# Routing a mixture of experts tile by tile, with places that need no totals

## The chip, the cores and the metric

The kernel runs on one core of a Trainium2 chip. The metric is the device time of one execution in microseconds. Before the change it is 1632.67 us, the median of three runs (1632.34 to 1632.82). The engines are named as in the profile: PE is TensorE, DVE is VectorE, ACT is ScalarE, POOL is GpSimd, SP is SyncE, which here only issues DMAs.

## What is computed

The input is 4096 tokens of 128 numbers (4 sequences of 1024), all in float32. Four parts follow one another:

```python
a = L0_attn(x)                    # linear attention, LayerNorm, gated FFN of width 341, LayerNorm
m = a + sum_e down_e(silu(a @ Wg_e) * (a @ Wu_e))   # 8 experts, all of them for each token, width 512
z = layernorm(m)                  # "n3": input of the second half
z4 = four layers(z)               # each: LayerNorm, quaternion products, filter, projection, LayerNorm, MLP of width 512
bid = sigmoid(z @ conf_w.T + conf_b) * wealth       # router: 8 numbers a token
top 2 of bid, weights softmax(bid[top 2])
y = sum over the 2 chosen e of weight * down_e(silu(z @ gate_e.T) * (z @ up_e.T))
out = m + z4 + y
```

The last part, the routed experts, needs only z and the router's numbers and not the result of the four layers, so the two can run side by side. With two experts a token there are 8192 rows to be computed, sorted by expert.

## The kernel before, in words

The tokens lie transposed in SBUF (feature on the partition, token along the row), in 8 tiles of 512 (`TILES`); a tile is 4 groups of 128 tokens (`GROUPS`). A planner written in the file decides the order of the work: `schedule` declares every step with the engines that it uses, a length in us, an urgency and the steps that it must follow (`step(...)`), some with resources that one step takes and another gives back (banks 6 and 7, the buffers YF and XS, the ACT table). `Plan.run` lays out the steps and gives each engine a fixed order. At run time each engine goes through its own order and waits on semaphores; nothing is reordered. The constants in capitals (NORM3, START, LATE, PACE) set urgencies, in units of one expert step.

*First stage, 256 expert steps.* For each tile, 32 steps (8 experts of 4 chunks): gate and up products of one chunk (L1231 to L1233, three passes each), silu on ACT (L780), product on DVE (L1110), down product into bank 4 (L1243). Between them lies the attention of the first half and, from the first finished tile on, the four layers of each tile: the products on DVE are `ham` (L1003 is the first of 13, L1009 to L1020 the others), the last addition of a layer is L1206.

*Normalisation.* `scaling` is used for every LayerNorm: PE centres four groups (L1321), ACT squares them (L789), POOL takes the power -0.5 (L953, step `power`), ACT copies the four groups scaled into rows of tokens (L802, step `scale`), PE turns them back (L1327, step `turn`). For the kind `n3` the rows are written to ROWS3, which is the buffer YF; SP stores them into the DRAM tensor xrows (step `rows`, L676), and only then is YF free for `ffn2_add` of the next tile. PE forms the router's logits from z (L1374), ACT copies them into LG (L865), 32 columns a tile.

*Routing, once for all tokens.* After tile 7, `route` runs for all 4096 tokens on DVE with 256 columns an operation (L1041 to L1062: bias, sigmoid by a Tanh on ACT, best and second best of 8). Each DVE operation is tied to the one before by `link` (a semaphore). PE counts how often each expert is chosen and ranks each token within its expert (L1415 to L1426). DVE turns the totals into the end of each expert's share, in blocks of 256 rows (`BLOCK`), and from end and rank into PLACE, the row of each token and choice (L1065 to L1079), then into OWNER, the expert of each of the 39 blocks (L1081 to L1084), then the weights. SP loads the rows of all tokens back from xrows into TOKROWS, and `columns` adds to each row its destination and its weight. POOL scatters them (step `scatter`, L959): 64 indirect DMAs of 128 rows of 520 bytes into the DRAM tensor xg, whose 9984 rows SP has filled with empty rows beforehand in three transfers (step `fill`, L671).

*Last stage, 39 blocks.* SP loads a block's weights by the expert in OWNER (`load_w`, behind the semaphore `placed`) and its 256 rows (`load_x`, behind all 64 scatters). PE transposes the rows (`turn_in`, L1436), ACT copies them, PE forms gate and up (L1447), ACT silu, DVE product, PE down (L1458), ACT scales by the weight, POOL scatters the results to ytok by the destination in the row (L970). After the last block, `load_y`, `back` (L1468), `merge` (L1222) and `out` bring them into the output, tile by tile.

## Time and profile before

| | us |
|---|---|
| median of 3 runs | 1632.67 |
| lowest, highest | 1632.34, 1632.82 |
| profiled execution, its time | 1633.69 |
| profiled execution, its span | 1631.9 |
| PE busy | 1478.9 (91% of the span) |
| DVE busy | 1144.5 (70%) |
| ACT busy | 1021.3 (63%) |
| POOL busy | 339.9 (21%) |
| DMA | 208.74 MB, 128 GB/s on average |

The span is the time between the first and the last instruction that the profiler saw; the profiled execution's own time is 1.8 us longer. Busy shares are averages over stages: which engine sets the time must be read stage by stage, from the slices and windows. The slices cut the span into 40 pieces of 40.8 us. The granted clock is what the chip allowed PE in that stretch; 1.00 is its upper level, 2.4 GHz, and values in between are a mix with the lower one, 1.2 GHz.

### The profile page before, as it was taken

To read this page: it belongs to the slowest core of one execution; us is meant where nothing else is said; L and a number is where in the kernel's file an instruction comes from. 1 tells how busy PE (TensorE), PEld (TensorE's weight loads), DVE (VectorE), ACT (ScalarE), POOL (GpSimd) and SP (SyncE) were. 2 spreads that over 40 slices of the span, in tenths; PEclk is the share of its full clock that TensorE was granted. 3 is DMA by queue.
4 is the path that set the end of the run, shared out by engine and by line. 5 is a ranking of instruction groups with operands and counts; after the bars stand their busy time and mean duration, and the time that the engine had idled before them with its cause. 6 is when DMAs were issued, how large, how long until landed. Compare 5 with 4: busy or idle time off the path is not lost.

```text
span 1631.9 us, 20218 instructions
## 1 busy us (share of the span) xinstructions
PE 1478.9 (91%) x6166; PEld 975.7 (60%) x6166; DVE 1144.5 (70%) x1222; ACT 1021.3 (63%) x2447; POOL 339.9 (21%) x253
## 2 busy tenths in 40 slices
PE   6999999998999999999999999996656999999996
PEld 4766566565555655555565566553323667677885
DVE  3433745948999359947993899799888798857221
ACT  6455657568666684677667667566636876655430
POOL 0001001101101111100011011013887233344231
PEclk9999999999999999999999999998769999999998
DMA  5733343334344244243432434325423354445455
GB/s 204 268 123 118 118 159 105 115 112 159 107 126 131 87 115 131 84 122 100 126 100 89 137 103 121 108 68 173 112 73 90 115 149 146 144 129 177 145 162 164
DMA packets 114853, 208.74 MB, mean 128 GB/s; under 512 B 13815, under 2 KB 61772, under 8 KB 113452
## 3 DMA queue, kind: packets, MB, share of 16 engines
q1 hardware_dynamic: 110204, 198.09, 39.7%
q0 software_dynamic: 4544, 9.38, 1.7%
q8 instruction: 51, 0.84, 0.2%
q14 instruction: 54, 0.44, 0.1%
HBM read 158.20 MB, written 29.24 MB: 115 GB/s over the span
## 4 chain that ended last, share of the span: by engine, by line
PE 34%; issue 28%; DVE 14%; ACT 12%; POOL 11%; DMA 1%; POOLq 0%; SPq 0%; ACTq 0%; DVEq 0%
PE bank L1243 6%; PE bank L1231 4%; PE bank L1233 4%; PE bank L1232 4%; POOL xg L959 4%; POOL ytok L970 4%; POOL RSTD L953 3%; PE bank L1409 3%; ACT ROWS L789 3%; PE bank L1321 3%; DVE TA L1009 2%; PE bank L1403 2%; DVE SH L1110 2%; DVE AM L1013 2%; DVE AM L1017 2%
## 5 line engine op out<-in xcount | busy, mean ns | idle before, releaser
L953 POOL TENSOR_TENSOR RSTD<-SS,power_half 128x4 f32<-128x4 f32 x96 | 139.4, 1452 | 952.4 <-ACT ROWS L789 952.1
L1110 DVE TENSOR_TENSOR SH<-SH,bank 128x512 f32<-128x512 f32 x256 | 172.8, 682 | 154.7 <-ACT SH L780 109.3
L1231 PE MATMUL bank<-NH,GU 128*128 128x512 f32 x512 | 266.9, 521 | 5.1 <-DVE SH L1110 2.9
L1243 PE MATMUL bank<-SH,WD 128*128 128x512 f32 x512 | 261.5, 593 | 0.1
L1009 DVE TENSOR_TENSOR TA<-QK 128x2048 f32<-128x2048 f32 x96 | 219.6, 2287 | 1.3
L780 ACT ACTIVATE SH<-bank 128x512 f32<-128x512 f32 x256 | 151.4, 601 | 110.0 <-PE bank L1233 106.7
L789 ACT ACTIVATE ROWS<-bank,root_eps 128x128 f32<-128x128 f32 x384 | 135.8, 367 | 123.4 <-PE bank L1321 123.1
L1233 PE MATMUL bank<-NL,GU 128*128 128x512 f32 x512 | 204.1, 399 | 0.0
L1232 PE MATMUL bank<-NH,GU 128*128 128x512 f32 x512 | 203.2, 397 | 0.0
L802 ACT ACTIVATE ROWS<-bank,RSTD 128x128 f32<-128x128 f32 x384 | 109.8, 372 | 78.1 <-POOL RSTD L953 72.0
L1013 DVE TENSOR_TENSOR AM<-AM,TA 128x1024 f32<-128x1024 f32 x128 | 152.9, 1217 | 0.6
L1447 PE MATMUL bank<-XT,GU 128*128 128x256 f32 x624 | 146.7, 381 | 3.3 <-ACT XT L929 3.3
L970 POOL DMA_INDIRECT ytok<-YS,XR x78 | 97.9, 1255 | 212.4 <-ACT YS L941 199.8
L1403 PE MATMUL bank<-XS,FC 128*128 128x512 f32 x256 | 126.5, 617 | 11.2 <-ACT GE L916 8.2
L1231 PEld LDWEIGHTS bank<-NH,GU 128*128 128x128 f32 x512 | 97.2, 190 | 54.6 <-issue 34.7
L1447 PEld LDWEIGHTS bank<-XT,GU 128*128 128x128 f32 x624 | 113.7, 190 | 20.8 <-ACT XT L929 5.0
L1232 PEld LDWEIGHTS bank<-NH,GU 128*128 128x128 f32 x512 | 98.0, 191 | 45.6 <-issue 33.2
L1215 DVE TENSOR_TENSOR SH<-SH,bank 128x512 f32<-128x512 f32 x78 | 52.9, 683 | 101.3 <-PE bank L1447 54.3
L1409 PE MATMUL bank<-GE,MP 128*128 128x512 f32 x256 | 119.2, 610 | 2.4 <-ACT GE L916 2.0
L1383 PE MATMUL bank<-XS,WQ 128*128 128x512 f32 x192 | 99.2, 626 | 14.7 <-ACT QK L877 11.7
L1243 PEld LDWEIGHTS bank<-SH,WD 128*128 128x128 f32 x512 | 96.6, 189 | 24.9 <-DVE SH L1110 0.9
L1233 PEld LDWEIGHTS bank<-NL,GU 128*128 128x128 f32 x512 | 96.6, 189 | 22.6
(197 smaller groups left out, 2492.7 us busy)
## 6 DMA issues: line engine op xcount, KB each, us to landing
GU<-halves SPq DMA_DIRECT2D x112, 512.0 KB, 3.9
GU<-in_w_gu SPq DMA_DIRECT2D x39, 512.0 KB, 3.7
WD<-in_w_d SPq DMA_DIRECT2D x128, 128.0 KB, 2.2
QK<-QK SPq DMA_DIRECT2D x32, 480.0 KB
WD<-in_w_d SPq DMA_DIRECT2D x39, 256.0 KB, 3.9
halves<-GU SPq DMA_DIRECT2D x8, 1024.0 KB, 6.3
FC<-ready_w SPq DMA_DIRECT2D x32, 256.0 KB, 3.9
MP<-in_w_mproj SPq DMA_DIRECT2D x32, 256.0 KB, 4.0
```

What stands on the lines that cost most here:

```text
L789: ins = act.activation(ROWS[:, i, :], LNB[:, i * P:(i + 1) * P], ACT.Square, bias=root_eps[:], scale=P ** -0.5, accum_out=SS[:, i:i + 1])
L953: pool.tensor_tensor(RSTD[:], SS[:], (power_one if k[0] == "at" else power_half)[:], ALU.pow).then_inc(power_done, 1)
L970: pool.indirect_dma_start(ytok, bass.IndirectOffsetOnAxis(ap=to, axis=0), YS[:, g % 2, j, :], None).then_inc(y_stored[i], 16)
L1009: ins = dve.tensor_tensor(TA[:], q, k_(1 + i // 3), ALU.mult)
L1013: ins = dve.tensor_tensor(pair(AM, *d), pair(AM, *d), pair(TA, *s), op)
L1110: dve.tensor_tensor(SH[:, g % 4, :], SH[:, g % 4, :], banks[2 + g % 2][:], ALU.mult).then_inc(h_ready, 1)
L1231: pe.matmul(out, w_hi, x_hi, start=True, stop=False)
L1232: pe.matmul(out, w_lo, x_hi, start=False, stop=False)
L1233: return pe.matmul(out, w_hi, x_lo, start=False, stop=True)
L1243: pe.matmul(banks[4][:], WD1[:, slot, :], SH[:, g % 4, :], start=first, stop=last).then_inc(down_done, 1)
L1409: mm = pe.matmul(banks[7][:], MP[:, c, :], GE[:, c, :], start=(c == 0), stop=(c == 3))
L1447: mm = pe.matmul(banks[bank][:, c * BLOCK:(c + 1) * BLOCK], GU[:, g % DEEP, a:a + P], XT[:, i, :], start=True, stop=True)
```

## The change

Each tile is routed as soon as its logits are there (step `route` with the tile in its key, four stages), and its 8 indirect DMAs go out at once. To need no totals, each expert gets 4096 rows of its own in xg (`c_base`, loaded into OFF, is expert number times 4096). BASE, the next free row of each expert, starts there and grows by the tile's counts; a token's place is BASE plus its rank in the tile. The ranks are 4 accumulating matmuls of 32 columns (one with the triangle `tri`, three with ones for the groups before), and 4 of 8 columns give the tile's totals. The Exp of the weights stays on ACT, once a tile. ACT writes the n3 rows twice, into SEND0 (in YF) and into SEND, one copy for each choice, each with room for its destination and weight; xrows, TOKROWS, `columns`, `load_rows` and the tables btri and of_expert are gone. xg has 34560 rows and not 9984; SP fills it in 8 transfers of 4096 rows, each before its tile's scatters, and a last one of 1792 rows. YF is free for the next tile's `ffn2_add` when the tile's 8 scatters have landed. After tile 7, `block_table` computes on DVE from the totals which expert each block has (OWNER) and at which row of xg it begins (ROW0), behind a small load of block numbers that SP issues after the last routing; `load_x` reads the start from there into a register. The last stage waits for these and for all scatters. The planner gets the new steps and lengths and other values for some of its constants; `prep` (the layers' weights) is put at other places.

The core of the diff:

```diff
+            step("power", k, urgency, [(POOL, 1.4)], [("centre", k, ACT_)])
+            step("scale", k, urgency, [(ACT_, 2.0 if kind == "n3" else 1.0, ("YF",) if kind == "n3" else ())], [("power", k, POOL)])
...
-    for i in range(-(-BLOCKS * BLOCK // TOK)):
-        step("fill", i, SPAN * (i + 2), [(SP, 0.1)], [("expert", (i + 2, 0), PE)])
+    for t in range(TILES):
+        step("fill", t, SPAN * t - 18, [(SP, 0.1)], [("expert", (t - 1, 4), PE) if t else ("raw", EXPERTS - 1, SP)])
...
-    ATTN = (-7.31, 18.93)
-    NORM1 = (2.85, 60.26)
-    FFN2 = (67.27, -54.82)
-    NORM2 = (29.18, 38.61)
-    NORM3 = (-31.42, 13.09)
+    ATTN = (-7.21, 18.93)
+    NORM1 = (4.12, 60.26)
+    FFN2 = (67.27, -48.32)
+    NORM2 = (9.93, 112.4)
+    ROUTE = (4.0, 3.97)
+    NORM3 = (-32.06, -2.73)
...
-             [("ffn2", (t, c), DVE) for c in range(3)] + last("ffn2_down", PE) + ([("rows", t - 1, SP, 3.0)] if t else []))
+             [("ffn2", (t, c), DVE) for c in range(3)] + last("ffn2_down", PE) + ([("scatter", (t - 1, 7), POOL, 3.0)] if t else []))
...
-        step("rows", t, a + NORM3[h], [(SP, 0.1, (), ("YF",))], [("turn", ("n3", t), PE)])
...
+        step("logits", t, a + NORM3[h] + 4.0, [(PE, 0.9, ("6",)), (ACT_, 0.1, (), ("6",))],
+             [("normed", ("n3", t), ACT_)] + ([("route", (t - 1, 3), DVE)] if t else []))
+        r = a + NORM3[h] + ROUTE[h]
+        step("route", (t, 0), r, [(DVE, 0.15), (ACT_, 1.4, ("table",), ("table",))], [("logits", t, ACT_)])
+        step("route", (t, 1), r, [(DVE, 3.3)], [("route", (t, 0), ACT_)])
+        step("route", (t, 2), r, [(PE, 1.4, ("6",)), (ACT_, 1.4, ("table",), ("table",), (), -1.4)], [("route", (t, 1), DVE)])
+        step("route", (t, 3), r, [(DVE, 2.5, (), ("6",))], [("route", (t, 2), ACT_), ("route", (t, 2), PE)])
+        for i in range(2 * GROUPS):
+            step("scatter", (t, i), r + 0.01 * i, [(POOL, 1.45, (), ("YF",) if i == 7 else ())],
+                 [("route", (t, 3), DVE), ("fill", t, SP, 14.0)])
...
-    LATE, PACE = 236.33, 2.81
-    ROUTE = -500.0
-    step("load_rows", 0, ROUTE, [(SP, 0.3)], [("rows", TILES - 1, SP, 3.0), ("logits", TILES - 1, ACT_)])
...
-    step("route", 3, ROUTE, [(PE, 0.9)], [("route", 2, ACT_, -2.4)])
-    step("route", 4, ROUTE, [(DVE, 6.0)], [("route", 3, PE), ("route", 2, ACT_)])
-    step("route", 5, ROUTE, [(POOL, 0.3)], [("scatter", NG - 1, POOL, 2.5)])
-    for j in range(2 * NG):
-        step("scatter", j, ROUTE + 0.01 * j, [(POOL, 1.6)], [("load_rows", 0, SP, 12.0), ("route", 5, POOL) if j >= NG else ("route", 4, DVE)])
+    LATE, PACE = 236.33, 0.74
+    step("load_numbers", 0, -500, [(SP, 0.1)], [("route", (TILES - 1, 3), DVE)])
+    step("table", 0, -500, [(DVE, 4.9)], [("load_numbers", 0, SP, 2.5)])
...
+        step("load_w", g, u - 9, [(SP, 0.8)], [("table", 0, DVE)] + ([("down", g - DEEP, PE)] if g >= DEEP else []))
+        step("load_x", g, u - 3, [(SP, 0.4)], [("table", 0, DVE), ("scatter", (TILES - 1, 7), POOL, 3.0)] + ([("y_store", (g - DEEP, 1), POOL, 2.0)] if g >= DEEP else []))
...
+    xg = nc.dram_tensor("xg", (SENT, P + 2), F32, kind="Internal").ap()
...
-                at = slice(k * TOK, min((k + 1) * TOK, BLOCKS * BLOCK))
-                sp.dma_start(xg[at, :], A["c_fill"][at, :]).then_inc(filled, 16)
+                if k >= 2:
+                    sp.wait_ge(filled[k % 2], 16 * (k // 2))
+                some = [x[0:EXPERTS * TOK, :].rearrange("(e r) n -> e r n", e=EXPERTS)[:, k * TILE:(k + 1) * TILE, :]
+                        for x in (xg, A["c_fill"])]
+                sp.dma_start(*some).then_inc(filled[k % 2], 16)
+                if k == TILES - 1:
+                    sp.dma_start(xg[EXPERTS * TOK:, :], A["c_fill"][EXPERTS * TOK:, :]).then_inc(rest_filled, 16)
...
-            elif name == "rows":
-                sp.wait_ge(rows_scaled, upto("scale", ("n3", k)))
-                sp.dma_start(xrows[k * TILE:(k + 1) * TILE, :].rearrange("(g p) n -> p g n", p=P), ROWS3[:]
-                             ).then_inc(rows_stored, 16)
...
-                sp.wait_ge(rows_stored, 16 * TILES)
-                sp.dma_start(TOKROWS[:, :, 0:P], xrows.rearrange("(j p) n -> p j n", p=P)).then_inc(tokrows_loaded, 16)
+            elif name == "load_numbers":
+                sp.wait_ge(routed, TILES)
+                sp.dma_start(block_no[:], A["c_block_no"][:, 0:BLOCKS]).then_inc(numbers_loaded, 16)
...
                 sp.wait_ge(scattered, 16 * 2 * NG)
+                sp.wait_ge(rest_filled, 16)
+                sp.wait_ge(table_set, 1)
                 if k >= DEEP:
                     sp.wait_ge(x_turned, k - DEEP + 1)
                     sp.wait_ge(y_stored[i], 16 * 2 * (k // DEEP))
-                sp.dma_start(XR[:, i, :, :], xg[k * BLOCK:(k + 1) * BLOCK, :].rearrange("(i p) n -> p i n", p=P)
+                r = sp.value_load(ROW0[0:1, k:k + 1], min_val=0, max_val=SENT - BLOCK)
+                sp.dma_start(XR[:, i, :, :], xg[bass.ds(r, BLOCK), :].rearrange("(i p) n -> p i n", p=P)
                              ).then_inc(xr_loaded[i], 16)
...
-                    dst = ROWS3
-                    act.wait_ge(rows_stored, 16 * k[1])
+                    dst = SEND0
+                    act.wait_ge(scattered, 16 * 2 * GROUPS * k[1])
                     act.wait_ge(centred, upto("centre", ("n2", k[1])))
                 act.wait_ge(turned_back, n)
                 for i in range(GROUPS):
-                    ins = act.activation(dst[:, i, :], LNB[:, i * P:(i + 1) * P], ACT.Copy, scale=RSTD[:, i:i + 1])
+                    ins = act.activation(dst[:, i, 0:P], LNB[:, i * P:(i + 1) * P], ACT.Copy, scale=RSTD[:, i:i + 1])
+                    if k[0] == "n3":
+                        ins = act.activation(SEND[:, i, 0:P], LNB[:, i * P:(i + 1) * P], ACT.Copy, scale=RSTD[:, i:i + 1])
                 ins.then_inc(rows_scaled, 1)
...
-                pool.wait_ge(filled, 16 * -(-BLOCKS * BLOCK // TOK))
-                pool.wait_ge(tokrows_loaded, 16)
-                i, j = k // NG, k % NG
-                pool.wait_ge(columns_set, i + 1)
-                pool.indirect_dma_start(xg, bass.IndirectOffsetOnAxis(ap=PLACE[:, i, j:j + 1], axis=0),
-                                        TOKROWS[:, j, :], None).then_inc(scattered, 16)
-            elif name == "route" and k == 5:
-                pool.wait_ge(scattered, 16 * NG)
-                columns(pool, 1)
+                t, i = k
+                c, g = i // GROUPS, i % GROUPS
+                pool.wait_ge(filled[t % 2], 16 * (t // 2 + 1))
+                pool.wait_ge(routed, t + 1)
+                rows = SEND0 if c == 0 else SEND
+                pool.indirect_dma_start(xg, bass.IndirectOffsetOnAxis(ap=PLACE[:, c, g:g + 1], axis=0),
+                                        rows[:, g, :], None).then_inc(scattered, 16)
...
+            elif stage == 3:
+                dve.wait_ge(ranked, t + 1)
+                rank = banks[6][:, 0:GROUPS * EXPERTS].rearrange("p (g e) -> p g e", e=EXPERTS)
+                link(dve.tensor_tensor(SLOT[:], rank, wide(BASE[:]), ALU.add))
+                total = banks[6][:, GROUPS * EXPERTS:(GROUPS + 1) * EXPERTS]
+                dve.tensor_tensor(BASE[:], total, BASE[:], ALU.add).then_inc(rank_read, 1)
+                link(dve.tensor_tensor(PICKED[:], ONE[:], SLOT[:].unsqueeze(1).broadcast_to([P, 2, GROUPS, EXPERTS]), ALU.mult))
                 link(dve.tensor_reduce(PLACEF[:], PICKED[:], AX.X, ALU.add))
+                dve.wait_ge(scattered, 16 * 2 * GROUPS * t)
+                dve.wait_ge(rows_scaled, upto("scale", ("n3", t)))
                 dve.tensor_copy(PLACE[:], PLACEF[:])
-                shape = [1, BLOCKS + 1, EXPERTS]
-                link(dve.tensor_tensor(PAST[:], block_no[:].unsqueeze(2).broadcast_to(shape),
-                                       end[0:1, EXPERTS:].unsqueeze(1).broadcast_to(shape), ALU.is_ge))
-                link(dve.tensor_reduce(OWNERF[:], PAST[:], AX.X, ALU.add))
-                dve.tensor_scalar(OWNER[:], OWNERF[:], EXPERTS - 1.0, None, ALU.min).then_inc(placed, 1)
-                dve.wait_ge(exp_done, 1)
+                for c, rows in ((0, SEND0), (1, SEND[:])):
+                    dve.tensor_copy(rows[:, :, P].bitcast(mybir.dt.uint32), dest[:, c, t * GROUPS:(t + 1) * GROUPS])
+                dve.wait_ge(exp_done, t + 1)
                 link(dve.tensor_scalar(SUM[:], EX[:], 1.0, None, ALU.add))
-                link(dve.reciprocal(WEIGHT[:, 0, :], SUM[:]))
-                link(dve.tensor_tensor(WEIGHT[:, 1, :], EX[:], WEIGHT[:, 0, :], ALU.mult))
-                columns(dve, 0)
+                link(dve.reciprocal(SEND0[:, :, P + 1], SUM[:]))
+                dve.tensor_tensor(SEND[:, :, P + 1], EX[:], SEND0[:, :, P + 1], ALU.mult).then_inc(routed, 1)
...
+        def block_table():
+            dve.wait_ge(numbers_loaded, 16)
+            dve.wait_ge(rank_read, TILES)
+            for e in END:
+                dve.memset(e[:], 0.0)
+            link(dve.tensor_tensor(FILL[:], BASE[:], OFF[:], ALU.subtract))
+            link(dve.tensor_scalar(FILL[:], FILL[:], 1.0 / BLOCK, (BLOCK - 1.0) / BLOCK - 0.5 + 0.5 / BLOCK, ALU.mult, ALU.add))
+            link(dve.tensor_scalar(FILL[:], FILL[:], ROUND, None, ALU.add))
+            link(dve.tensor_scalar(FULL[:], FILL[:], ROUND, None, ALU.subtract))
+            link(dve.tensor_copy(END[0][:, EXPERTS:], FULL[:]))
+            for i, d in enumerate((1, 2, 4)):
+                a, b = END[i % 2], END[(i + 1) % 2]
+                link(dve.tensor_tensor(b[:, EXPERTS:], a[:, EXPERTS:], a[:, EXPERTS - d:2 * EXPERTS - d], ALU.add))
+            link(dve.tensor_scalar(FILL[:], FULL[:], -float(BLOCK), float(TOK), ALU.mult, ALU.add))
+            shape = [1, BLOCKS, EXPERTS]
+            link(dve.tensor_tensor(PAST[:], block_no[:].unsqueeze(2).broadcast_to(shape),
+                                   END[1][0:1, EXPERTS:].unsqueeze(1).broadcast_to(shape), ALU.is_ge))
+            link(dve.tensor_tensor(SKIP[:], PAST[:], FILL[0:1, :].unsqueeze(1).broadcast_to(shape), ALU.mult))
+            link(dve.tensor_reduce(OWNERF[:], PAST[:], AX.X, ALU.add))
+            link(dve.tensor_reduce(ROW0F[:], SKIP[:], AX.X, ALU.add))
+            link(dve.scalar_tensor_tensor(ROW0F[:], block_no[:], float(BLOCK), ROW0F[:], ALU.mult, ALU.add))
+            dve.tensor_copy(ROW0[:], ROW0F[:])
+            dve.tensor_scalar(OWNER[:], OWNERF[:], EXPERTS - 1.0, None, ALU.min).then_inc(table_set, 1)
...
-                dve.wait_ge(rows_stored, 16 * k)
+                dve.wait_ge(scattered, 16 * 2 * GROUPS * k)
...
+            elif name == "route":
+                pe.wait_ge(chosen, k[0] + 1)
+                bank_free(pe, 6, name, k)
+                out = banks[6][:, 0:GROUPS * EXPERTS]
+                every = ones[:, 0:1].broadcast_to([P, P])
+                pe.matmul(out, tri[:], CHOSEN[:, GROUPS - 1:, :].rearrange("p g e -> p (g e)"), start=True, stop=False)
+                for d in range(1, GROUPS):
+                    at = slice(GROUPS - 1 - d, 2 * GROUPS - 1 - d)
+                    pe.matmul(out, every, CHOSEN[:, at, :].rearrange("p g e -> p (g e)"), start=False, stop=(d == GROUPS - 1))
+                for g in range(GROUPS):
+                    mm = pe.matmul(banks[6][:, GROUPS * EXPERTS:(GROUPS + 1) * EXPERTS], every, CHOSEN[:, GROUPS - 1 + g, :],
+                                   start=(g == 0), stop=(g == GROUPS - 1))
                 mm.then_inc(ranked, 1)
...
-                pe.wait_ge(placed, 1)
+                pe.wait_ge(o_added, TILES)
```

## Rows read from the trace of the kernel before

**Rows 1.** The page, busy tenths and granted clock in 40 slices of the span.

```profile
PE   6999999998999999999999999996656999999996
...
PEclk9999999999999999999999999998769999999998
```

**Rows 2.** Windows: length, then busy us and instructions of each engine, clock, DMA share, GB/s.

```profile
0.00:1100.00 1100.00, 1034.52 (x4078) 661.36 (x4078) 777.11 (x841) 723.96 (x1731) 111.53 (x85) 1.00 0.40 124
...
900.00:1100.00 200.00, 190.90 (x696) 116.85 (x696) 177.54 (x178) 131.93 (x321) 20.51 (x14) 0.99 0.37 110
...
1140.00:1270.00 130.00, 83.64 (x218) 38.13 (x217) 114.67 (x98) 73.14 (x183) 101.42 (x71) 0.80 0.35 98
1270.00:1600.00 330.00, 314.73 (x1633) 241.89 (x1632) 211.20 (x220) 197.35 (x459) 114.34 (x88) 1.00 0.47 143
```

**Rows 3.** Lines L959 (scatters) and L1436 (transposes of blocks): min/median/max ns, first and last start.

```profile
L959 POOL DMA_INDIRECT xg<-TOKROWS,PLACE x64: 955/1055/2971, 1132.0 to 1260.3; - x64
...
  issue: 17.1, 59
...
DMA to landing us min/median/max: 2.3/3.2/7.3
...
L1436 PE MATMUL bank<-ident,XR x78: 272/273/327, 1269.0 to 1592.4; 128*128 128x128 f32 x78
```

**Rows 4.** Timeline of the last tile's scaling, logits and routing: start us, us, engine, line.

```profile
1104.38 1.14 ACT L802 ACTIVATE attn_raw<-bank,RSTD 128x128 f32<-128x128 f32 x4 [0.16 <-POOL RSTD L953]
...
1107.92 0.96 PE L1374 MATMUL bank<-conf,Z 128*128 128x8 f32 x8
...
1109.80 0.21 ACT L865 ACTIVATE LG<-bank 128x32 f32<-128x32 f32 x1
...
1116.33 0.19 DVE L1057 TENSOR_TENSOR DIF<-M 128x32 f32<-128x32 f32 x1
...
1125.96 0.57 DVE L1071 TENSOR_TENSOR END<-END 128x8 f32<-128x8 f32 x3
```

**Rows 5.** Block loads, last block matmuls, layer products (L1003) and a layer's last addition (L1206).

```profile
XR<-xg SPq DMA_DIRECT2D x39, 130.0 KB, 2.3
...
L1458 PE MATMUL bank<-WD,SH x624: 272/275/377, 1287.9 to 1601.2; 128*128 128x128 f32 x156
...
1131.02 2.29 DVE L1003 TENSOR_TENSOR AM<-QK 128x2048 f32<-128x2048 f32 x1
...
1419.47 2.29 DVE L1003 TENSOR_TENSOR AM<-QK 128x2048 f32<-128x2048 f32 x1 [0.34 <-ACT V L907]
...
1483.18 2.29 DVE L1003 TENSOR_TENSOR AM<-QK 128x2048 f32<-128x2048 f32 x1 [0.94 <-ACT V L907]
...
L1206 DVE SCALAR_TENSOR_TENSOR Z<-bank,LC,Z x32: 737/746/753, 235.9 to 1534.4; 128x512 f32<-128x512 f32 x32
```

**Rows 6.** ACT's table loads, and what PE waited for (whole span, to 1100, 1130 to 1270).

```profile
101.64 1.28 ACT L780 ACT_TABLE_LOAD   x1
102.94 1.09 ACT L780 ACTIVATE SH<-bank 128x512 f32<-128x512 f32 x2
...
L780 ACT ACT_TABLE_LOAD x36 | 46.2, 1283 | 0.6
...
L925 ACT ACT_TABLE_LOAD x1 | 1.3, 1283 | 0.0
...
L1231 PE MATMUL bank<-NH,GU 128*128 128x512 f32 x512 | 266.9, 521 | 5.1 <-DVE SH L1110 2.9 <-ACT SH L780 2.2
...
PE bank L1327 <- ACT ROWS L802: 20.3, 21, 6.5
...
PE bank L1327 <- ACT ROWS L802: 21.8, 8, 6.5
```

**Rows 7.** The fills: their size and landing time, and the window behind the first one.

```profile
xg<-in_c_fill SPq DMA_DIRECT2D x2, 2080.0 KB, 10.4
...
225.00:235.00 10.00, 10.00 (x33) 5.62 (x32) 2.54 (x4) 8.27 (x17) 1.01 (x1) 1.00 0.91 319
```

195 lines of the change are left out of this document (70 added, 125 removed).

## The prediction

> **What bounds the kernel now.** The slices come first [rows 1]: TensorE (PE) reads 9 almost everywhere, except in the first slice, in slices 28 to 31 (about 1101 to 1264 us), where it reads 6, 6, 5, 6 and the granted clock falls to 7 and 6, and in the last. TensorE is the bound; there is one hole. The windows give it numbers [rows 2]: from 0 to 1100 us PE is busy 1034.5 of 1100 us (94.0%), from 1270 to 1600 us 314.7 of 330 (95.4%), but from 1140 to 1270 us only 83.6 of 130, at a mean granted clock of 0.80. Next, the one line that runs in the hole and nowhere else [rows 3]: 64 scatters on POOL, the first at 1132.0 us, the last at 1260.3, and the first transpose of a block of the last stage at 1269.0. No block of that stage may start before all 64 have landed, and they cannot start before all eight tiles are routed. In the meantime PE has only the attention layers, a chain that VectorE (DVE) carries: it is busy 114.7 of the 130 us. So the hole is not spare time of a slow engine. It is matmul work of 39 blocks, locked behind POOL's scatters, while PE idles. What ends last there is the scatter chain.
>
> **What the change does to the hole.** Of 64 scatters, 56 move to where their tiles are finished, before 1100 us; 8 are left behind the last tile. I build the new start of the last stage from the old times of the last tile. Its logits reach SBUF at 1109.8+0.2 us [rows 4]. The scaling in front of them issues eight copies where it issued four; four take 1.14 us [rows 4], so +1.1. Routing is then 16 DVE operations up to CHOSEN; one of 32 columns took 0.19 us, and three small linked ones 0.57 [rows 4]; at 0.20 us that is 3.2. The ranks are 8 matmuls, each two instructions in the trace; the logits' matmuls, as narrow, took 0.96 us for 8 instructions [rows 4], so 1.9 for 16. Ten DVE operations follow, 2.0. Eight scatters at 0.96 us and 0.30 of issue [rows 3] take 10.1; landing is 3.2 [rows 3], the load of a block 2.3 [rows 5]. With 1 us for handovers that is 1134.8. DVE is in order and its layer operations of 2.29 us stand between the routing steps [rows 5]: two of them, 4.6. First block at about **1140 us instead of 1269**. The block table (about 20 DVE operations, some 5 us) and the first weights behind it lie beside the scatters. If that cover is gone, they cost those 5 us once.
>
> From there the remaining PE work is the same. Full-clock work is busy time times granted clock: 83.6 x 0.80 = 66.9 us in the rest of the hole, and 314.7 up to 1600 us, together 381.6 [rows 2]. At the 95.4% of the late stage this takes 400.1 us, so the last block's last matmul, at 1601.5 us now [rows 5], comes at 1140 + 400.1 + 1.5 = 1541.6. The tail behind it (last stores, load back, transposes, output) does not change. **Term A: -60 us.** Does DVE allow it? It has 114.7 + 211.2 = 326 us to do in 401 us, 81%. From 900 to 1100 us it ran at 89% with PE at 95% [rows 2], so yes. The layers' last addition is at 1534.4 us now [rows 5], and need not come sooner. Ten of the eleven layers left start their products from 1131.0 to 1419.5 us [rows 5], on average 32 us apart: 29 in the hole (four steps up to 1247.4), 34.4 beside blocks. The last starts 64 us later and ends 51 after that. At 34.4 throughout it ends at 1131 + 9 x 34.4 + 64 + 51 = 1555.6. Behind the layers come some 15 us of output, behind the blocks 30 (1601.5 to 1631.9), so the two ends are even. The bounds of A are -65 (PE at 97%) and -45 (layers late by 15 us).
>
> **What the change adds before 1100 us.** PE: the ranks, 16 instructions and 1.92 us for each of 7 tiles, 13.4 us on the engine that is the bound. They are no filler for idle time, since that time is waits at handovers of an ordered queue. **Term B: +13.4 us** (bounds 0, all in gaps, and 14).
>
> ScalarE: four more copies a tile (1.1 us), one Tanh, one Exp. The Tanh of now has no table load in the trace; the Exp has one [rows 6]. So I count two loads a tile (Exp, and silu again), 14 in all. A load lasts 1.283 us, and the copy after it starts 0.02 us behind its end [rows 6]. PE waited 2.9 + 2.2 us in all for the silu and its product, with 36 returns to silu [rows 6], 0.14 us each: 14 x 0.14 = 2.0. The Trainium skill ("ScalarE: Activation LUTs", section "What ACT_TABLE_LOAD costs") says that a switch costs the 1.283 us and a drain of 1.38 us besides. By it the 14 switches would hold ScalarE 37 us and not 18; the trace has the load as stated and no gap behind it, so the sum goes without the drain.
>
> POOL: 56 scatters of 1.26 us. POOL is busy 111.5 of 1100 us [rows 2], so there is room, but its other work is the power step in the middle of every normalisation, and PE's transpose waits behind that: 20.3 us in 21 waits up to 1100 us [rows 6]. A power caught behind one scatter is late by 1.26 us at most; I take one or two a tile, half of it passed on: 7 x 0.6 = 4. The doubled copies lengthen one of the tile's normalisations by 1.1 us; about every third of them makes PE wait (21 waits, some 80 normalisations), so 7 x 1.1 x 0.3 = 2. **Term C: +8 us** (2 + 4 + 2). Its lower bound is 0. Its upper bound is the hole: there PE waited 21.8 us for ROWS beside 64 scatters [rows 6], so 19 for 56; with all the added copies (8) and 2 for tables, 29.
>
> DVE: 26 operations a tile at 0.2 us, 5.2 us, 37 us in seven tiles; it is busy 777 of 1100 us, 71%, and becomes 74%. Nothing, while it stays under the 89% that it has from 900 to 1100 us [rows 2]. Against that the 12 us of routing 4096 tokens at once near 1110 to 1131 us shrink to 5.
>
> DMA: the empty rows written beforehand grow from 5.2 to 18 MB, in eight fills of 2.1 MB, where there were two [rows 7] and a short one. I cost them at nothing: in the window right behind the first fill the DMA share was 0.91 and PE was busy 10.00 of 10 us [rows 7], as weights are loaded several steps ahead. A fill takes 10.4 us to land [rows 7]; if that cover is gone (the first one falls into the start-up), 5 to 10 us once. The 8 row stores, the reload of 2 MB and the five tables behind it go away; the first block's load waits no more for them. On SyncE each block gets one register load more, 39 in all, hidden behind a block's matmuls (some 6 us).
>
> **Sum.** -60 + 13.4 + 8 = -38.6 on the profiled execution (1633.69 us, its span 1631.9). The median of the runs shown is 1632.67, a microsecond lower; from it, **1594 us**.
>
> **Rivals.**
>
> *Costs hidden.* B and C fall into the 65 us of PE's idle time before 1100 us, and A reaches -63: 1632.7 - 63 = 1570. For it: the planner orders the steps and can put ranks where PE waits. Against: PE has waits of 1 to 2 us there, each already in a dependency. Chance 0.14.
>
> *The hole closes only in part.* The layers become the bound after 1140 us: two chains of four layers each, DVE at 81%, and their short matmuls now queue on PE among those of the blocks. If they come every 37 us, the last addition is at 1131 + 9 x 37 + 64 + 51 = 1579, the end some 15 us later, 1594; B and C, which shift all of it, make 1615. For it: 34.4 us apart beside blocks, and 64 for the last. Against: there they had room to wait, since the blocks set the end. Chance 0.15.
>
> *Slower, by buffer YF.* The rows of a tile now lie in YF until its eight scatters have landed; before, a single store of them freed it. The next tile's ffn2_add on DVE waits for them, and behind it in DVE's queue stand the experts' products, hence PE. The planner knows of this, with 1.45 us a scatter; in the hole the longest took 2.97 [rows 3]. Where scatters run 1.5 us long, a tile's eight are 12 us late. From 5.5 us of stall a tile on (38.6 / 7) the gain is gone; at 10 us, 1594 + 70 = 1664. For it: POOL's work did stretch in the hole. Against: a tile lasts 137 us, in which 10 to 25 us of scatters find room, and POOL idled there 90%. Chance 0.05.
>
> *The last stage does not start early.* A wait keeps it (the last fill, the rows' order), or the order written by the planner puts layer steps first, and only B and C (+21.4) are left against what a POOL free of scatters can return of PE's waits for ROWS in the hole (-21.8, [rows 6]): 1632, within 0.2%. Chance 0.04; 0.62 stays for the forecast.
>
> **How the numbers follow.** The forecast's own range is 1577 to 1610 (A and C within two thirds of their bounds). The whole range of 8 in 10 reaches down to the first rival and into the second: 1567 to 1620. A difference of 0.2%, 3.3 us, is about what a measurement of this kernel can tell from no change. Faster by more: 0.62 + 0.14 + 0.15, and a bit of the last, 0.92; the same 0.02; slower 0.06.
>
> **What would show it.** Right: 56 scatters spread over 130 to 1090 us and 8 near 1120 to 1132; first block transpose at about 1160 (B and C shift it by some 20 us); granted clock 9 in every slice but the last; last block matmul near 1560; ranks at 1.9 us a tile. Wrong in A: layers' last addition behind the last block, PE idle beside it. Wrong in C: in the waits, PE for ROWS well above 25 us before 1100, or DVE waiting for the scatters. Wrong in DMA: PE waiting for weights.

## The result, and the profile after

Four runs of the changed kernel gave a median of 1597.62 us (1592.25 to 1601.19), four of the kernel before beside them 1632.74 us: a ratio of 0.977, with a 95% interval of 0.974 to 0.979 (the quotient of the two medians, 0.9785, lies inside it). The forecast of 1594 us is 4 us off. Its parts are not as good as their sum. The profiled execution of after took 1592.25 us (span 1590.4), 5 us under its median; the runs of this kernel spread more than those of before (9 us against 4), so the windows below explain a difference of 41.5 us between two spans, and the medians one of 35. Times in this document are medians of executions at the usual granted clock (a mean of 0.96 to 0.99 over the span), and two slower ones, of scat2 (2172 us at 0.65) and of the kernel before beside it (1692 us at 0.88), are left out.

The page of the changed kernel, its busy time and the slices that answer to [rows 1]:

```profile
span 1590.4 us, 20945 instructions
...
PE 1480.2 (93%) x6278; PEld 988.1 (62%) x6278; DVE 1167.9 (73%) x1414; ACT 1039.9 (65%) x2503; POOL 341.8 (21%) x251
...
PE   6999999999999999999999999999779999999978
...
PEclk9999999999999999999999999999889999999989
```

The hole of four slices has become one of two, 7 and 7. A dip in the granted clock is left there (8 and 8), and there is a new soft spot at the very end, 7 and 8 with a clock of 8 and 9.

The windows of after, cut at its last experts' addition (1111.4 us; the addition that ends the first stage's expert work for tile 7), its first block transpose (1179.8) and its last block matmul (1535.3); the columns are those of [rows 2]:

```profile
0.00:1111.40 1111.40, 1050.94 (x4192) 678.70 (x4192) 800.00 (x1020) 743.64 (x1782) 186.39 (x141) 0.99 0.42 136
1111.40:1179.80 68.40, 47.91 (x151) 24.84 (x152) 58.08 (x90) 44.85 (x122) 19.10 (x14) 0.80 0.36 107
1179.80:1535.30 355.50, 340.79 (x1745) 258.01 (x1744) 276.17 (x274) 236.04 (x562) 131.24 (x92) 1.00 0.48 146
1535.30:1590.40 55.10, 40.53 (x195) 26.59 (x193) 33.64 (x35) 15.35 (x39) 5.03 (x4) 0.90 0.43 133
```

And the kernel before, cut at the same event of its own, its last experts' addition at 1099.3 us, and at its first block transpose:

```profile
0.00:1099.30 1099.30, 1034.15 (x4077) 661.23 (x4078) 776.41 (x840) 723.67 (x1730) 111.53 (x85) 1.00 0.40 124
1099.30:1269.00 169.70, 110.23 (x317) 54.19 (x316) 150.38 (x155) 98.64 (x254) 112.04 (x78) 0.81 0.39 111
```

These windows divide the difference in two. By the last experts' addition both kernels have done nearly the same layer work (the last additions of 19 layers lie before it in both), and after is 12.1 us late. From there to the end of the span before needs 532.6 us (1631.9 - 1099.3) and after 479.0: 53.6 us less. 12.1 - 53.6 = -41.5, the difference of the spans. The prediction had +21.4 and -60.

Four lines of after, with the first and last start of each: the additions of the experts, the blocks' transposes, the blocks' last matmuls (down product), and the layers' last additions.

```profile
L1119 DVE SCALAR_TENSOR_TENSOR X<-bank,cols,X x8: 742/746/751, 126.6 to 1111.4; 128x512 f32<-128x512 f32 x8
...
L1440 PE MATMUL bank<-ident,XR x78: 272/273/330, 1179.8 to 1515.3; 128*128 128x128 f32 x78
...
L1462 PE MATMUL bank<-WD,SH x624: 272/275/423, 1193.5 to 1535.3; 128*128 128x128 f32 x156
...
L1211 DVE SCALAR_TENSOR_TENSOR Z<-bank,LC,Z x32: 739/744/752, 239.9 to 1585.7; 128x512 f32<-128x512 f32 x32
```

In before the blocks ended 66.8 us behind the layers [rows 5]. Now the layers end 50.4 us behind the blocks, and the span ends 4.7 us after their last addition.

### The profile page after: what moved, and what is told of

It is laid out like the page before. It is cut to its first block, busy times and chain, and to the rows that moved or that the text cites. A ratio compares the mean times of both kernels' runs of the same rounds, so it can differ in the third digit from the quotient of the medians.

```text
span 1590.4 us, 20945 instructions
## 1 busy us (share of the span) xinstructions
PE 1480.2 (93%) x6278; PEld 988.1 (62%) x6278; DVE 1167.9 (73%) x1414; ACT 1039.9 (65%) x2503; POOL 341.8 (21%) x251
## 3 DMA queue, kind: packets, MB, share of 16 engines
q1 hardware_dynamic: 105020, 206.60, 41.5%
## 4 chain that ended last, share of the span: by engine, by line
PE 43%; issue 19%; DVE 15%; ACT 15%; POOL 4%; DMA 3%; SPq 1%; POOLq 0%; ACTq 0%; DVEq 0%
PE bank L1250 6%; PE bank L1416 4%; PE bank L1238 4%; PE bank L1240 4%; PE bank L1239 4%; PE bank L1410 4%; PE bank L1328 3%; ACT ROWS L781 3%; POOL RSTD L945 2%; PE bank L1451 2%; ACT ROWS L794 2%; DVE AM L1003 2%; PE bank L1390 2%; DVE SH L1115 2%; DVE TA L999 2%
## 5 line engine op out<-in xcount | busy, mean ns | idle before, releaser
L1115 DVE TENSOR_TENSOR SH<-SH,bank 128x512 f32<-128x512 f32 x256 | 171.8, 682 | 129.0 <-ACT SH L772 89.2
L772 ACT ACTIVATE SH<-bank 128x512 f32<-128x512 f32 x256 | 151.4, 602 | 98.6 <-PE bank L1240 95.9
L1003 DVE TENSOR_TENSOR AM<-AM,TA 128x1024 f32<-128x1024 f32 x128 | 153.0, 1218 | 0.8
L960 POOL DMA_INDIRECT ytok<-YS,XR x78 | 108.5, 1390 | 162.2 <-ACT YS L933 149.2
L1334 PEld LDWEIGHTS bank<-ident,ROWS 128*128 128x128 f32 x384 | 45.3, 144 | 88.0 <-ACT ROWS L794 71.1
```

The costliest lines, as they stand in the source:

```text
L1003: ins = dve.tensor_tensor(pair(AM, *d), pair(AM, *d), pair(TA, *s), op)
L1115: dve.tensor_tensor(SH[:, g % 4, :], SH[:, g % 4, :], banks[2 + g % 2][:], ALU.mult).then_inc(h_ready, 1)
```

## Where the last tile's time goes

The forecast put the first block 41 us behind the last experts' addition; it came 68.4 us behind. The timeline of after in that stretch (start, duration, engine, line):

```profile
1111.36 0.74 DVE L1119 SCALAR_TENSOR_TENSOR X<-bank,cols,X 128x512 f32<-128x512 f32 x1
...
1119.15 2.08 PE L1328 MATMUL bank<-centre,X 128*128 128x128 f32 x8 [1.02 <-ACT XS L827]
...
1128.62 0.68 ACT L819 ACTIVATE Z<-bank 128x512 f32<-128x512 f32 x1
1128.96 3.67 PE L1416 MATMUL bank<-GE,MP 128*128 128x512 f32 x8 [0.59 <-ACT GE L910]
...
1136.33 0.20 ACT L860 ACTIVATE LG<-bank 128x32 f32<-128x32 f32 x1 [0.41 <-PE bank L1381]
...
1144.57 0.19 DVE L1052 TENSOR_TENSOR CHOSEN<-ONE 128x32 f32<-128x32 f32 x1
...
1149.96 0.38 PE L1424 MATMUL bank<-CHOSEN,tri 128*128 128x32 f32 x2
...
1153.36 0.17 DVE L1070 TENSOR_TENSOR SEND<-EX,attn_raw 128x4 f32<-128x4 f32 x1
...
1155.78 1.06 POOL L952 DMA_INDIRECT xg<-attn_raw,PLACE  x1 [0.18 <-issue]
...
1166.98 0.96 POOL L952 DMA_INDIRECT xg<-SEND,PLACE  x1 [0.30 <-issue]
...
1174.25 4.43 SPq L724 DMA_DIRECT2D XR<-xg  x4
...
1179.78 0.38 PE L1440 MATMUL bank<-ident,XR 128*128 128x128 f32 x2
```

The durations of most single operations are as forecast: 0.16 to 0.22 us on DVE, 1.9 us for the ranks. A scatter took 0.96 to 1.95 us where 0.96 was counted; in [rows 3] that is the shortest, the median is 1.055. Step by step:

| stretch | measured, us | counted, us |
|---|---|---|
| addition to logits in SBUF (1136.5) | 25.2 | 11.8 |
| to CHOSEN (1144.8) | 8.2 | 3.2 |
| to the first rank matmul (1149.96) | 5.2 | 0 |
| to the first scatter (1155.78) | 5.8 | 3.9 |
| to the end of the eighth scatter (1167.94) | 12.2 | 10.1 |
| to the load of the blocks' rows (1174.25) | 6.3 | 3.2 |
| to the first transpose (1179.78) | 5.5 | 2.3 |
| handovers, and DVE's layer work between the steps | in the rows above | 5.6 |
| sum | 68.4 | 40.1 (40.7 with 1139.4 rounded to 1140) |

What the sum lacked is mainly time in queues. After's written order puts a layer's centring, projections and transposes ahead of the tile's own centring (1119.15), and more of a layer's products ahead of the logits. DVE does layer operations between the routing steps, for which the 5.6 us were meant. From CHOSEN to the ranks PE does projections of a layer and waits for its ROWS. The first scatter stands behind a power operation of a layer on POOL. The last transposes ahead of the first block wait 2.3 us for a layer's ROWS, while the block's rows had landed 2.2 us after their issue. Such queues make 28.7 us more in five of the rows (13.4 + 5.0 + 5.2 + 1.9 + 3.2), against the 5.6 that were allowed: 23.1 of the 27.7 us missed. The rest is the scatters' length (2.1) and the landing of the last one (3.1, less 0.6 of rounding). SP stood 3.5 us waiting for that landing:

```profile
SPq L723 <- DMA xg<-SEND,PLACE: 3.5, 1, 3.5
```

The forecast counted 3.2 us for it, and it took about 6. Just before it SP had issued the weights of the first four blocks (3.1 MB, 1164.23 to 1169.44 us), and from 1168 to 1174 us the DMA engines were busy all the time, at 357 GB/s. No run moved these loads, so that they delayed the landing is likely and not shown.

## Experiments

All ratios are to the kernel before on the same chip, with 95% intervals. A kernel that was to price the doubled copies of the n3 rows (copy2, four more ACT copies a tile) needs more SBUF than there is and has no time, so their cost by itself is not measured.

**late100: does the gain come from the early start?** The schedule is told that the numbers for the block table arrive 100 us later. It writes its orders by that, and nothing else changes.

```diff
...
-    step("table", 0, -500, [(DVE, 4.9)], [("load_numbers", 0, SP, 2.5)])
+    step("table", 0, -500, [(DVE, 4.9)], [("load_numbers", 0, SP, 102.5)])
```

> The kernel after, where the planner is told that the block table is ready 100 us later, so that the order of each engine has layer steps first and the blocks start about as late as before the change; all instructions and waits are the same. If the early start of the blocks is the gain (term A, 60 us) and the early routing costs the 12 us by which the last experts' addition came later (1111 against 1099), this gives back the gain and keeps the cost: 1635-1655. Rival 'POOL free of scatters speeds the layers up in the hole' : the layers run faster without scatters, and it stays at 1600-1625.

Measured: 1657.18 us, ratio 1.012 [1.009, 1.015]. The experts' last addition was at 1110.3 us, as in after; the blocks' lines:

```profile
L1440 PE MATMUL bank<-ident,XR x78: 272/273/473, 1286.2 to 1617.8; 128*128 128x128 f32 x78
...
L1462 PE MATMUL bank<-WD,SH x624: 272/275/377, 1311.1 to 1626.7; 128*128 128x128 f32 x156
```

The first block starts 106.4 us later than in after and the last matmul ends 91.4 us later. So with a late start the gain is gone; it is the start of the blocks, as term A said. That POOL without scatters might speed the layers up in the hole is refuted: the hole is there again (PE busy 116.0 of the 175.9 us between the experts' last addition and the first block), with POOL busy for only 32.1 us of it. The loss of some 20 us is more than the 12 us of the change's early cost, and 2 us above the expected range: the first block came 17.2 us later than in before (1286.2 against 1269.0).

**pace281 and pace16: which end sets the time?** The change also set PACE, the distance at which blocks are due in the schedule, from 2.81 to 0.74 us.

```diff
-    LATE, PACE = 236.33, 0.74
+    LATE, PACE = 236.33, 2.81
```

That is pace281, which takes the value of before; pace16 has 1.6 there and pace18 (below) 1.8.

> The kernel after, with the planner's PACE back at 2.81 (0.74 after the change); it gives the blocks less urgency against the layer steps, and touches nothing else. In the profile of after the blocks end at 1535 us and the layers' last addition only at 1586, so I now hold that the layers set the end. Theory 'layers bound the end': the last addition moves forward to about 1530-1545, the blocks' last matmul back to about 1555-1565, the whole gains 5 to 15 us on after (about 1583-1592). Rival 'PE's work bounds the end': the two ends swap places and the time stays within 3 us of after, 1598. Rival 'planner constants carry the gain': it loses, 1605 or more.

> The kernel after with PACE 1.6, between the two. Theory 'layers bound the end': both ends come within 20 us of each other, and the time is the lowest of the three, 1580-1588. Rival 'PE's work bounds the end': within 3 us of after.

pace281: 1612.27 us, 0.986 [0.984, 0.987]; pace16: **1587.58 us, 0.971 [0.969, 0.972]**, below the changed kernel's 0.977 [0.974, 0.979]. The expectation for pace281 failed: the ends moved as its first theory said (layers' end earlier, blocks' end later) but the blocks' end overshot, to 1577.2 and not 1565, and the time rose by 15 us where it was to fall by 5 to 15. It lies in the range of the third theory, that the new planner constants carry part of the gain; see oldplan. Their ends, blocks' last matmul and layers' last addition:

```profile
L1462 PE MATMUL bank<-WD,SH x624: 272/275/421, 1190.5 to 1577.2; 128*128 128x128 f32 x156
...
L1211 DVE SCALAR_TENSOR_TENSOR Z<-bank,LC,Z x32: 739/744/753, 240.6 to 1547.0; 128x512 f32<-128x512 f32 x32
```

```profile
L1462 PE MATMUL bank<-WD,SH x624: 272/275/377, 1191.6 to 1553.3; 128*128 128x128 f32 x156
...
L1211 DVE SCALAR_TENSOR_TENSOR Z<-bank,LC,Z x32: 739/744/751, 239.3 to 1563.2; 128x512 f32<-128x512 f32 x32
```

The first fence is pace281, the second pace16; in both the blocks set the end, in pace16 by 15 us, in after the layers do. Each span is the later of two ends, by a rule read off these traces: the blocks' last matmul plus 30 us, or the layers' last addition plus 5 us. pace281 gives 1577.2 + 30 = 1607 (span 1607.6), pace16 1553.3 + 30 = 1583 (1582.6), after 1585.7 + 5 = 1591 (1590.4). The rule fits within 2 us in every trace of this document.

> The changed kernel with PACE 1.8 instead of 0.74, that is blocks due 1.8 us apart. If the end is set by the later of the blocks' last matmul plus 30 us and the layers' last addition plus 5 us, the trace of PACE 1.6 (blocks 1553.3 us, layers 1563.2 us) has the blocks' end as the later one already, and more pace moves the blocks later still: 1588 to 1600 us. If the balance still leans to the layers there, 1580 to 1586 us.

pace18 gave 1590.54 us, 0.974 [0.971, 0.977]. Its blocks ended earlier than with 1.6, at 1546.1, and its layers later, at 1584.1 (+ 5 = 1589, span 1588.8). The rule held; the expectation that a larger PACE moves the blocks later was wrong: the time is in its range, but the other end makes it. The planner lays out many steps one after another, and a small change of one constant moved the ends either way.

**rank2: what do the rank matmuls cost?** They are issued twice.

```diff
+                for twice in range(2):
-                pe.matmul(out, tri[:], CHOSEN[:, GROUPS - 1:, :].rearrange("p g e -> p (g e)"), start=True, stop=False)
+                    pe.matmul(out, tri[:], CHOSEN[:, GROUPS - 1:, :].rearrange("p g e -> p (g e)"), start=True, stop=False)
...
```

> The kernel after with each tile's 8 rank matmuls issued twice (16 instructions and 1.9 us more a tile, same result). If term B is a full cost on the bound engine, the last experts' addition comes 7 x 1.9 = 13 us later (1124) and the whole 13-15 us later (1611-1613). If PE's idle time before 1100 us takes them in, the addition moves by under 5 us and so does the whole.

1617.19 us, 0.988 [0.986, 0.991], 4 us above the expected range. The window up to its last addition:

```profile
0.00:1131.40 1131.40, 1072.09 (x4304) 698.10 (x4304) 800.17 (x1019) 743.27 (x1782) 182.55 (x141) 0.98 0.42 133
```

Against the window of after the addition is 20.0 us later and PE 21.15 us busier, for 112 more instructions (16 in each of seven tiles) that cost 13.4 us at full clock. Idle time absorbed next to nothing of it (59.3 us idle, 60.5 in after). The other 7.7 us, which the expectation lacked, go with a lower granted clock (mean 0.98 against 0.99). Cut the first 1100 us into windows of 10 us, and for each multiply its 10 us by what its granted clock lacks to 1.00: the sum, time lost by the clock, is 3.5 us in before, 8.5 in after and 17.1 in rank2. A cluster of ranks often stands behind a pause of PE; the section on the hardware shows one.

**only8: what does the hole cost by itself?** The kernel before, with 8 of its 64 scatters (56 are left out, so most rows of the blocks are empty ones; the blocks compute as long as ever) and a write of 4 MB to the outputs' buffer ahead of time.

```diff
...
-    for j in range(2 * NG):
+    for j in range(8):
...
```

> The kernel before, with 8 of the 64 scatters (the other 56 left out, so most tokens get no routed experts; the places they would have been read from are filled beforehand, 4 MB more); the blocks all run, on mostly empty rows, and the planner knows of the 8. Nothing is added before 1100 us. Theory 'the 56 scatters behind tile 7 are what holds the blocks': the first block comes at about 1160 and not 1269, and the time is 1565-1580, the gain of term A alone. Rival 'something else holds the blocks' (the reload of all rows, the weights, the order): under 20 us of gain, 1613 or more.

1589.77 us, 0.974 [0.971, 0.978]. First block at 1168.8 us instead of 1269.0, blocks' end at 1556.3 instead of 1601.5, the layers' last addition at 1543.0. The first block is 100 us earlier and the blocks' end 45: term A measured without the rest of the change. (The last addition is at 1106.2 us, 6.9 later than in before: PE has one wait of 7.7 us more, up to 394.5 us. The profile names no releaser for it; the added write went out at 366.0.) Behind that addition the kernel needs 480.2 us (1586.4 - 1106.2) instead of 532.6: the early start by itself is worth 52.4 us, nearly the 53.6 of the change. Its expectation, 1565 to 1580 us, was too low, by about as much as the first block was later than the 1160 us expected; 6.9 us of that are the addition's delay.

**scat2, scat15, scat2plan: do the scatters hold up the normalisations?** Every scatter is sent a second time, to a spare buffer; in scat15 only those of the first choice (c == 0); in scat2plan all, and the schedule is told, which is the second hunk.

```diff
+                pool.indirect_dma_start(xg2, bass.IndirectOffsetOnAxis(ap=PLACE[:, c, g:g + 1], axis=0),
+                                        rows[:, g, :], None).then_inc(spare, 16)
...
-            step("scatter", (t, i), r + 0.01 * i, [(POOL, 1.45, (), ("YF",) if i == 7 else ())],
+            step("scatter", (t, i), r + 0.01 * i, [(POOL, 2.9, (), ("YF",) if i == 7 else ())],
```

> The kernel after with each of the 64 scatters issued twice, the second time into another DRAM tensor (10 us more of POOL a tile; the planner does not know). Theory 'early scatters hide in POOL's idle time': the last experts' addition stays within 3 us of 1111, and only the last tile's 8 scatters show, 10 us: 1603-1610. Rival 'scatters hold up the normalisations' (the cost put at 4 us in term C, or the YF rival): the addition moves by 10 us or more, and the whole to 1615 or more.

> The changed kernel with the scatters of the first choice alone sent twice, the second time to a spare buffer: 12 scatters a tile instead of 8 (16 a tile moved the last experts' addition from 1111.4 us to 1170.5 us). If each scatter in front of a power operation costs the layer normalisations the same amount, the addition moves by half of that, to about 1141 us, and the time by about 30 us, to 1627 us; and then the 8 scatters that the change itself makes would have cost about 59 us, which its trace does not have. If POOL has room for the scatters up to some number and only more than that holds TensorE up, the cost is bent: under 12 us, an addition before 1124 us and a time of 1600 to 1612 us.

> The changed kernel with each scatter sent twice, as in scat2, and the schedule's scatter step told to last 2.9 us instead of 1.45, so that the written orders of POOL and TensorE are made for the doubled scatters. scat2 without this had its last experts' addition at 1170.5 us, 59 us behind the changed kernel, and TensorE waited 61.6 us for the scaled rows before 1100 us. If what the doubled scatters cost is POOL's time itself, the addition stays behind 1155 us and the waits for the scaled rows above 45 us. If it is that the order of the other engines was made for scatters of half the length, the addition comes back to 1110 to 1125 us, the waits to under 30 us, and the scatters of the change, which its schedule knows, cost next to nothing before the last addition. The time would then be 1600 to 1625 us (16 scatters of tile 7 lie ahead of the first block, and the ends of blocks and layers shift with the order).

scat2: 1656.91 us (three executions), 1.016 [1.012, 1.020], last addition at 1170.5. scat15: 1631.39 us, 0.997 [0.995, 0.999], addition at 1143.8. scat2plan: 1635.45 us, 1.000 [0.998, 1.002], addition at 1126.1. What PE waited for, up to 1100 us in after and scat2 and up to 1110 in scat2plan (us in total, times, longest):

```profile
PE bank L1334 <- ACT ROWS L794: 17.9, 21, 6.7
```

```profile
PE bank L1342 <- ACT ROWS L798: 61.6, 22, 10.0
```

```profile
PE bank L1342 <- ACT ROWS L798: 23.5, 15, 6.0
```

The line is PE's transpose waiting for rows that ACT scaled by POOL's power. scat2 refutes that early scatters always hide in POOL's idle time: sent without the schedule's knowledge they hold the normalisations up. Such scatters cost in proportion: 4 more a tile moved the addition by 32 us, 8 more by 59. So the bent cost that scat15 was to show isn't there, and the consequence that the change's own 8 scatters cost 59 us too isn't in the trace either. scat2plan tells why. With the same doubled scatters in a schedule that knows them, the waits fall from 61.6 to 23.5 us and the addition comes back by 44 of 59 us (1 us short of the expected range). It is the fixed order of the engines, made for shorter scatters, that costs most, not POOL's time. The whole kernel comes back by less, 21 of the 59 us between scat2 and the changed kernel, and missed its expected 1600 to 1625 us. Before the last stage PE stood 18.15 us in front of the first block, whose rows now lie behind 16 scatters of the last tile, and the layers' last addition came at 1627.6.

```profile
1197.46 0.69 PE L1448 MATMUL bank<-ident,XR 128*128 128x128 f32 x2 [18.15 <-DMA XR<-xg]
```

**oldplan: where is the cost that was forecast?** The changed kernel with the due times of before for the steps that both have: NORM2 as shown, and NORM0, KEYS, KV_SUM, ATTN, NORM1, FFN2, NORM3 and START likewise.

```diff
...
-    NORM2 = (9.93, 112.4)
+    NORM2 = (29.18, 38.61)
...
```

> The changed kernel with the due times of the kernel before for the steps that both have (NORM0, KEYS, KV_SUM, ATTN, NORM1, FFN2, NORM2, NORM3, START). If the 4.7 us of idle TensorE time that the change had less before the last experts' addition came from its new due times, that idle time is back and more: the addition at 1120 to 1132 us, TensorE idle for 70 us or more before it (60.5 us in the changed kernel), and a time of 1603 to 1615 us. If it came from the structure (no reload of the rows, no split of the chain), the addition stays at 1111 us within 3 us and the time within 5 us of 1595 us.

1614.5 us, 0.986 [0.982, 0.991]: a ratio 0.010 above the changed kernel's, 16 us. The last addition came at 1140.0 us, later than either theory had it, with PE idle for 67.9 us before it (1140.0 - 1072.13):

```profile
0.00:1140.00 1140.00, 1072.13 (x4253) 691.60 (x4254) 832.33 (x1047) 767.25 (x1838) 182.22 (x144) 0.99 0.42 134
```

PE had issued 61 more instructions by then, layer work done ahead. So most of the 28.6 us by which the addition is later is work moved forward and not lost: PE is 21.2 us busier (some 5 of it a lower clock, 13.6 against 8.5 by the sum used for rank2) and idle for 7.4 us more than in after (60.5), which is close to but under the 70 expected. The time is in the range of the theory that the new due times keep the idle time down. They are worth 16 us of time.

PACE (pace281, 15 us) and the due times (16 us) are both part of the change, whose whole gain is 35 us. They were not set back together, and the kernel before was not given a newly fitted schedule. So how the 35 us divide between structure and schedule is open. That the early start pays by itself is not: only8 gains 44 us with the old constants.

**fill2 and fill15: are the fills free?** Each fill (2080 KB) is followed by another, or by half of one, to a spare buffer.

```diff
...
+                some = [x[0:EXPERTS * TOK, :].rearrange("(e r) n -> e r n", e=EXPERTS)[:, k * TILE:(k + 1) * TILE, :]
+                        for x in (xg2, A["c_fill"])]
+                sp.dma_start(*some).then_inc(spare[k % 2], 16)
```

> The kernel after with each fill of empty rows made twice, the second time into another DRAM tensor (17 MB more read and written, none of it read back). If the fills are hidden behind weights loaded ahead, as I costed them: 1596-1601, the last experts' addition within 2 us of 1111. If they delay weights or the rows' scatters: 5 us or more for the whole.

> The changed kernel with half a fill more (1040 KB to a spare buffer, right behind each fill of 2080 KB); a whole fill more moved the last experts' addition from 1111.4 us to 1167.3 us. If TensorE's weights have a fixed cover that the first fill stays within (10.4 us of transfer, cover of 10 to 15 us by the loads that run ahead), half a fill goes past it in some tiles only: a time of 1600 to 1615 us, and waits for WD, GU or WQ of under 15 us before 1100 us. If each byte costs the same, the addition comes near 1139 us and the time near 1625 us.

fill2: 1649.69 us, 1.010 [1.008, 1.013], last addition at 1167.3. fill15: 1615.19 us, 0.988 [0.986, 0.991], addition at 1131.3. PE's waits for weights in fill2 up to 1100 us; before has none:

```profile
PE bank L1259 <- DMA WD<-in_w_d: 14.9, 2, 11.0
PE bank L1399 <- DMA WQ<-ready_w: 12.4, 1, 12.4
PE bank L1425 <- DMA MP<-in_w_mproj: 9.9, 1, 9.9
PE bank L1247 <- DMA GU<-halves: 7.1, 3, 3.4
```

In fill15 they are 4.9, 7.9, 4.3 and 1.7 us, 18.8 in all against 44.3. After has one:

```profile
PE bank L1390 <- DMA WQ<-ready_w: 2.2, 1, 2.2
```

Half a fill more costs 19.9 us of the last addition, a whole one 55.9, the second half nearly twice the first. So the cost does not go by the byte: weights loaded ahead cover the first fill and run out behind it, as the first theory of fill15 had it (its time is at the end of the expected range, its waits for WD, GU and WQ are 14.5 us where under 15 were expected). About a third of the cost falls into the start-up, where all 14.9 us of waiting for WD lie: the first experts' addition moved from 126.6 to 144.5 us in fill2 and to 132.6 in fill15. The single fill is at the edge: 2.2 us of waiting for a weight up to 1100 us. "Nothing" was right for the change, and had no reserve; 1 MB more would not have been free.

## Why the prediction was right, point by point

**What bounded before.** Right. late100 holds the start of the blocks back and loses the whole gain (1.012); only8 lets them start early in the old kernel and gains 2.6% (44 us).

**First block at 1140 plus the shift.** Wrong by 27.7 us. The step counted each operation once and two waits behind DVE's products, and took the rest of the chain as ready when its input was. It is a chain of some ten handovers through ordered queues full of layer work, on PE above all, whose order was not looked at; 23 us are that. It also read the shortest scatter (0.955 us) for the median (1.055).

**Term A, -60.** It measured -53.6, behind the last experts' addition, and got there by another way. With the real shift of 12.1 us the forecast puts the blocks' last matmul at 1541.6 + 12.1 = 1553.7. It came at 1535.3, although the blocks started 27.7 us later than forecast: the order gave them PE at once, so they took 355.5 us and not 400 (PE was busy 340.8 of them, 95.9%, at a clock of 1.00). The layers paid for that. Their last addition was to come by 1555.6 (1567.7 with the real shift) and came at 1585.7. Their products start at 1132.2 and for the last time at 1541.2 us, 409 us apart, where 9 x 34.4 + 64 = 374 was the step. "The two ends are even" is the sentence that failed: in the blocks' stretch the written order puts the blocks' work first. pace281, which changes nothing but that order, has the layers' last addition 38.7 us earlier, and DVE, which carries the layers, stood 26.0 us there before a block's product and waited for its silu, against 40.7 in after. Beyond that, which wait set the layers' pace was not isolated.

This is the rival in which the hole closes only in part; it had the mechanism, and its price of 1615 us was too high, since it kept the 21.4 us and gave the layers' end a tail of 15 us, which is 4.7 now that the blocks are done before it. The runs with other values of PACE show that an order between the two ends is worth another 10 us.

**Term B, +13.4.** Right in mechanism: doubled, the ranks cost their 13.4 us in full (rank2). A term was missing, the granted clock: PE's busy time up to the same addition grew by 16.8 us (1050.94 - 1034.15), 13.4 of it the ranks; the clock's lost time, 8.5 against 3.5 us, accounts for the rest and, within the reading, a little more.

**Term C, +8.** Wrong in size, and in sign on the trace: PE's idle time before the addition fell from 65.2 to 60.5 us, -4.7. Waits for SH were 1.4 us (before 5.1). Waits for scaled rows hardly moved. For ROWS they were 17.9 us (before 20.3). The rows of n3 have lines of their own, since they go to the buffer that the profile calls attn_raw, and in after to SEND too. Before's line, then after's:

```profile
PE bank L1327 <- ACT attn_raw L802: 4.3, 5, 2.3
```

```profile
PE bank L1334 <- ACT SEND L796: 5.4, 4, 2.4
```

Together that is 23.3 us in after against 24.6 in before. The table loads and doubled copies are there and hidden: 107 loads instead of 96, and the next operation of ACT starts within 0.02 us of a load's end, as in the one shown, in 106 of the 107.

```profile
1129.32 1.28 ACT L900 ACT_TABLE_LOAD   x1
1130.62 1.06 ACT L900 ACTIVATE QK<-TURNS 128x1024 f32<-128x1024 f32 x1
```

The Trainium skill ("ScalarE: Activation LUTs", section "What ACT_TABLE_LOAD costs") adds a drain of 1.38 us to each switch; this trace shows none, nor did the trace of before.

That POOL's scatters can hold the normalisations is shown (scat2); that they need not, where the order is made for them, is shown too (scat2plan). oldplan shows part of what the order paid: without the new due times PE idles 7.4 us more and the time is 16 us longer. The step that failed is to price added work against an order that was written for the old work.

**DMA at nothing.** Right for the change (2.2 us), and for the reason given: fill2 and fill15 show the cover by showing where it ends. How near that is, the prediction did not see.

The sum came out 4 us from the measurement partly by luck, because errors of opposite sign met. On the profiled execution B and C together were 9.3 us too dear and A 6.4 us too generous, and inside A a start 27.7 us too late met blocks that ran 44.6 us shorter. The rest of the difference is the spread of the runs. Two of its signs were off as well: the first transpose (1160 forecast, 1179.8 measured) and a granted clock of 9 in every slice but the last (there are two of 8 in the hole).

## What to carry to other kernels

Look for a stage that is locked behind a serial chain, and price its opening by the two ends that race afterwards, not by the idle time in the hole: the work that used the hole is late next, and the balance between both is set by a constant that is worth trying at several values (1597.6 to 1587.6 us here, for one number). In a kernel with orders written ahead by a planner, added work costs less if the planner knows it (15 us and not 59 up to the last addition for the same scatters), so an estimate must say which of the two it prices. In a chain from one stage to the next, count a queueing delay for every handover between engines with a fixed order; here such delays made 28.7 us of 68, where 5.6 were counted.

## What the runs showed of the hardware

The granted clock fell behind some short pauses of PE. In after PE waits 1.9 us for a sum of DVE, and the next stretch is at 0.66 (windows of 4, 2, 5 and 4 us):

```profile
205.00:209.00 4.00, 4.00 (x15) 2.31 (x13) 4.00 (x6) 1.20 (x2) 0.00 (x0) 1.00 0.33 101
209.00:211.00 2.00, 0.10 (x2) 0.02 (x1) 1.97 (x4) 0.00 (x0) 0.00 (x0) 1.00 0.57 190
211.00:216.00 5.00, 5.00 (x11) 3.17 (x12) 1.90 (x3) 0.60 (x1) 0.00 (x0) 0.66 0.00 0
216.00:220.00 4.00, 4.00 (x19) 2.79 (x18) 1.44 (x2) 0.60 (x2) 0.00 (x0) 1.00 0.68 198
```

From 212 to 215 us it is 0.50 of full speed, the lower of the clock's two levels (1.2 of 2.4 GHz), with PE busy throughout. So this pause of 1.9 us cost some 1.7 us more behind it (5 x 0.34). In rank2 it shows around the first ranks: PE busy 2.19 of 4 us, then 30 instructions, most of them narrow (8 or 32 columns), in 3 us at 1.00, then 8 us at a mean of 0.57:

```profile
150.00:154.00 4.00, 2.19 (x13) 1.38 (x12) 2.54 (x14) 3.94 (x8) 0.00 (x0) 1.00 0.67 253
154.00:157.00 3.00, 3.00 (x30) 3.00 (x29) 1.89 (x3) 2.94 (x5) 0.00 (x0) 1.00 0.28 109
157.00:165.00 8.00, 8.00 (x25) 5.94 (x25) 2.82 (x12) 4.35 (x15) 4.16 (x4) 0.57 0.15 30
```

Not every pause has such a dip, and no run here varied a pause alone, so this is a reading of traces and not an experiment.
